# Row maxima of a cross-attention kernel turned in 32 by 32 blocks on VectorE

## The reference: what is computed

```python
x = residual + mha(layernorm(x), layernorm(ctx), W_qkv, b_qkv, W_o, b_o)   # 8 heads of 64, 4096 queries, 3202 keys
  # scores = q @ k.T / 8 ; attn = softmax(scores) ; out = attn @ v ; out @ W_o.T + b_o
xn = layernorm(x)
U = (xn @ W_in.T + b_in) @ Bmat
s = silu(s @ A.T) + u_t                    # scan over the 4096 tokens, state of 64
x = x + states @ Cmat + (program_probs.mean(axis=1) @ W_prog.T + b_prog)
```

## Time and profile before

| | |
|---|---|
| median of 3 runs | 2271.17 us |
| the profiled execution, its own time | 2271.68 us |
| its span, from first to last instruction | 2269.6 us |
| TensorE (PE) busy | 2225.6 us, 98% |
| VectorE (DVE) busy | 1714.8 us, 76% |
| GpSimd (POOL) busy | 1584.3 us, 70% |
| ScalarE (ACT) busy | 1093.8 us, 48% |
| mean granted TensorE clock | 0.993 of full speed |

### The profile page before, as it was taken

The page is one execution under the profiler, slowest core; times in us unless marked ns, Lnnn a source line. Parts: engine busy times, 40 slices in busy tenths (PEclk is TensorE's granted clock), DMA queues, the critical chain, the costliest instruction groups (busy, mean ns, idle before and its releaser), DMA issues.

```text
span 2269.6 us, 36015 instructions
## 1 busy us (share of the span) xinstructions
PE 2225.6 (98%) x14120; PEld 1283.7 (57%) x14120; DVE 1714.8 (76%) x2087; ACT 1093.8 (48%) x1418; POOL 1584.3 (70%) x1038
## 2 busy tenths in 40 slices
PE   8999999999999999999999999999999999999987
PEld 8998865455555555555555555555555555545764
DVE  6866546888888888888888888888888888854766
ACT  4653334545444444444454444444444444453454
POOL 1200027888888888888888888888888888988322
PEclk9999999999999999999999999999999999999998
DMA  7750226777777777777777777777777777778733
GB/s 270 209 184 10 75 76 138 160 157 157 160 157 160 160 168 170 170 165 170 166 156 167 170 173 168 173 173 166 154 158 161 163 173 166 174 178 188 247 103 148
DMA packets 170090, 365.44 MB, mean 161 GB/s; under 512 B 28537, under 2 KB 75001, under 8 KB 169410
## 3 DMA queue, kind: packets, MB, share of 16 engines
q0 software_dynamic: 59904, 218.13, 47.1%
q1 hardware_dynamic: 110018, 145.02, 20.2%
HBM read 95.82 MB, written 49.04 MB: 64 GB/s over the span
## 4 chain that ended last, share of the span: by engine, by line
PE 96%; ACT 1%; DMA 1%; DVE 1%; issue 0%; POOL 0%; SPq 0%; POOLq 0%; DVEq 0%; ACTq 0%
PE ps L1473 34%; PE ps L1338 12%; PE ps L1452 8%; PE ps L1450 8%; PE ps L1454 8%; PE ps L1442 5%; PE ps L1301 4%; PE ps L1540 4%; PE ps L1309 3%; PE ps L1319 3%; PE ps L1273 1%; PE ps L1563 1%; PE ps L1483 1%; PE ps L1343 1%; DMA acca<-pt 1%; PE ps L1603 1%
## 5 line engine op out<-in xcount | busy, mean ns | idle before, releaser
L797 ACT ACTIVATE pt<-ps 128x1024 f32<-128x1024 f32 x800 | 777.5, 1021 | 890.9 <-PE ps L1454 882.2
L1001 DVE TENSOR_REDUCE mx_part<-ps 128x2 f32<-128x1024 f32 x768 | 938.3, 1222 | 339.2 <-PE ps L1338 339.2
L604 POOL TENSOR_TENSOR accp<-accp,pt 128x1024 f32<-128x1024 f32 x416 | 1034.1, 2486 | 209.4 <-ACT pt L797 204.6
L1473 PE MATMUL ps<-pt,v 128*64 128x512 f32 x3328 | 805.8, 605 | 0.0
L1090 DVE TENSOR_TENSOR ps<-ps,shb 128x1024 f32<-128x1024 f32 x403 | 493.2, 1224 | 46.0 <-PE ps L1454 46.0
L1473 PEld LDWEIGHTS ps<-pt,v 128*64 128x64 f32 x3328 | 201.9, 136 | 344.9 <-issue 338.8
L1338 PE MATMUL ps<-kk,qh 64*128 64x512 f32 x1520 | 344.6, 449 | 1.6 <-DVE mx_part L1001 1.6
L1338 PEld LDWEIGHTS ps<-kk,qh 64*128 64x128 f32 x1520 | 141.7, 183 | 341.0 <-DVE mx_part L1001 250.2
L1450 PE MATMUL ps<-qh,kk 64*128 64x512 f32 x1664 | 328.6, 390 | 1.7 <-ACT pt L797 1.7
L1452 PE MATMUL ps<-qh,kk 64*128 64x512 f32 x1664 | 329.0, 390 | 0.0
L1454 PE MATMUL ps<-ql,kk 64*128 64x512 f32 x1664 | 328.3, 389 | 0.0
(11 more groups left out here) (165 smaller groups left out, 1794.2 us busy)
## 6 DMA issues: line engine op xcount, KB each, us to landing
acca<-pt POOLq DMA_DIRECT2D x224, 512.0 KB, 5.0
accb<-pt POOLq DMA_DIRECT2D x160, 512.0 KB, 4.8
q_scratch<-kk SPq DMA_DIRECT2D x32, 512.0 KB, 4.3
acca<-accp POOLq DMA_DIRECT2D x32, 512.0 KB, 4.6
o_scratch<-ost SPq DMA_DIRECT2D x32, 512.0 KB, 3.1
og<-o_scratch SPq DMA_DIRECT2D x32, 512.0 KB, 5.9
shb<-m_scratch SPq DMA_DIRECT2D x31, 512.0 KB, 4.5
xs<-x SPq DMA_DIRECT2D x16, 512.0 KB, 6.1
```

Source lines behind the costliest of these rows:

```text
L604: nc.gpsimd.tensor_tensor(acc[:, :], acc[:, :], pt[n % PT_SLOTS][:, :], ALU.add).then_inc(added_p, 1)
L797: nc.scalar.activation(pt[n % PT_SLOTS][:, :], src, ACT.Exp, scale=SCALE).then_inc(exped, 1)
L1001: nc.vector.tensor_reduce(mx_part[w % 2][:, m % QT, :, m // QT], ps[:, b:b + 2, :], AX_X, ALU.max)\
L1473: ins = mm(ps[HD * h:HD * (h + 1), 6, :], v[:, t, f:f + HD], pt[n % PT_SLOTS][:, h * QB:(h + 1) * QB], start=(t == 0), stop=(t == NT - 1))
```

## The change

The 8 columns are turned on VectorE, in blocks of 32 by 32. `mx_row` becomes 128 by 32 (24 columns are cleared once), and behind the reduction VectorE waits for it and transposes into `mx_turn`; block i (partitions 32i to 32i + 31) then holds 8 rows of 32 queries. SP stores these with four DMAs, one for each block, each of 8 rows of 32 numbers (128 bytes), where one DMA stored 8 rows of 512 bytes. The transpose on TensorE, the copy on ScalarE and their semaphores are gone; the sign moves into `ones_row` (minus one) and into `add_shift` (subtract). `spread_sum` waits for `den_taken` instead, and TensorE waits for `max_taken` before unit 0.

```diff
-        mx_row = at("mx_row", [P, 2, QT], RR + 11776)
+        mx_row = at("mx_row", [P, 32], RR + 11840, F32R)
+        mx_turn = at("mx_turn", [P, 32], RR + 11872, F32R)
-        shift_row = at("shift_row", [2 * QT, P], RR + 11840, F32R)
             def send_shift(w):
-                sp.wait_ge(shift_ready, w + 1)
+                sp.wait_ge(max_ready, w + 1)
                 wait(sp, sh_loaded, 16 * (w - 1))
                 wait(sp, shb_loaded, 16 * (w - 2))
-                sp.dma_start(m_scratch[w % 2].rearrange("h (q k) -> (h q) k", k=P), shift_row[:, :].bitcast(F32)).then_inc(sh_stored, 16)
-                sp.wait_ge(sh_stored, 16 * (w + 1))
+                by_tile = m_scratch[w % 2].rearrange("h (q k) -> (h q) k", k=P)
+                for i in range(4):
+                    sp.dma_start(by_tile[:, 32 * i:32 * (i + 1)], mx_turn[32 * i:32 * i + 2 * QT, :].bitcast(F32)).then_inc(sh_stored, 16)
+                sp.wait_ge(sh_stored, 64 * (w + 1))
-            nc.gpsimd.memset(ones_row[0:1, :].bitcast(F32), 1.0)
+            nc.gpsimd.memset(ones_row[0:1, :].bitcast(F32), -1.0)
...
-            def shift(w):
-                act.wait_ge(max_turned, w + 1)
-                wait(act, sh_stored, 16 * w)
-                nc.scalar.activation(shift_row[:, :], ps[0:2 * QT, turn_bank(w), 0:P], ACT.Copy, scale=-1.0)\
-                    .then_inc(shift_ready, 1)
...
             def take_max(w, m):
                 if m == 0:
-                    wait(dve, max_ready, w - 1)
+                    wait(dve, row_ready, w - 1)
...
             def row_max(w):
+                if w == 0:
+                    dve.wait_ge(row_cleared, 1)
                 dve.wait_ge(max_taken, NM * (w + 1) if w else M_EARLY)
-                wait(dve, max_turned, w)
-                nc.vector.tensor_reduce(mx_row[:, :, :].rearrange("p h q -> p q h"), mx_part[w % 2][:, :, :, :], AX_X, ALU.max)\
-                    .then_inc(max_ready, 1)
+                nc.vector.tensor_reduce(mx_row[:, 0:2 * QT].rearrange("p (h q) -> p q h", h=2), mx_part[w % 2][:, :, :, :], AX_X, ALU.max)\
+                    .then_inc(row_ready, 1)
+                dve.wait_ge(row_ready, w + 1)
+                wait(dve, sh_stored, 64 * w)
+                nc.vector.transpose(mx_turn[:, :].bitcast(F32), mx_row[:, :].bitcast(F32)).then_inc(max_ready, 1)
                     if n == 9:
                         dve.wait_ge(parts_loaded, 32)
+                        nc.vector.memset(mx_row[:, :].bitcast(F32), 0.0).then_inc(row_cleared, 1)
-                nc.vector.tensor_tensor(ps[:, b:b + 2, :], ps[:, b:b + 2, :], shb[u % 2][:, :, :], ALU.add)\
+                nc.vector.tensor_tensor(ps[:, b:b + 2, :], ps[:, b:b + 2, :], shb[u % 2][:, :, :], ALU.subtract)\
                     .then_inc(shifted, 1)
-            def turn_max(w):
-
-                pe.wait_ge(max_ready, w + 1)
-                wait(pe, den_taken, w - 1)
-                if w == 0:
-                    pe.wait_ge(n_ready, 2 * NG)
-                nc.tensor.transpose(ps[0:2 * QT, turn_bank(w), 0:P], mx_row[:, :, :].rearrange("p h q -> p (h q)"), ident[:, :])\
-                    .then_inc(max_turned, 1)
             project_v(NG - 1, 0)
-            turn_max(0)
             project_v(NG - 1, 1)
             pe.wait_ge(k_ready, FC * C_G)
-            pe.wait_ge(shift_ready, 1)
+            pe.wait_ge(max_taken, M_EARLY)
             def spread_sum(u):
                 pe.wait_ge(added_a[u % 2], 16 * (len(A_TILES) + 1) * (u // 2 + 1))
-                if u + 1 < UNITS:
-                    pe.wait_ge(shift_ready, u + 2)
+                wait(pe, den_taken, u)
-                    if ahead and j == TURN_STEP:
-                        turn_max(u + 1)
```

More of the change, by code:

```diff
@@ L55, in maxima_of @@
     return [(i // NM, i % NM) for i in range(first, min(first + 2, NM * UNITS))]
-TURN_STEP = NJ - M_LEAD
 PAIR_ORDER = [2, 3, 0, 1]
@@ L138, in max_bank @@
     return 5 if (w, m) in EARLY else 4
-def turn_bank(w):
-    return 7 if w else 0
 def k_slot(w):
@@ L338, in build @@
         max_done = sem("max_done"); max_taken = sem("max_taken"); max_ready = sem("max_ready")
-        max_turned = sem("max_turned"); shift_ready = sem("shift_ready"); qx_loaded = sem("qx_loaded"); sh_loaded = sem("sh_loaded")
+        row_cleared = sem("row_cleared"); row_ready = sem("row_ready"); qx_loaded = sem("qx_loaded"); sh_loaded = sem("sh_loaded")
         scored = sem("scored"); sh_stored = sem("sh_stored"); shb_loaded = sem("shb_loaded")
@@ L575, in _ @@
             nc.gpsimd.memset(pad[0:KEYS - (NT - 1) * P, :], 0.0)
-            nc.gpsimd.memset(ones_row[0:1, :].bitcast(F32), 1.0)
-            nc.gpsimd.memset(ones_row[HD:HD + 1, :].bitcast(F32), 1.0).then_inc(ones_set, 1)
+            nc.gpsimd.memset(ones_row[0:1, :].bitcast(F32), -1.0)
+            nc.gpsimd.memset(ones_row[HD:HD + 1, :].bitcast(F32), -1.0).then_inc(ones_set, 1)
             pool.wait_ge(ones_set, 2)
@@ L768, in _ @@
                 high_k(C_G - 1, i)
-            shift(0)
             for t in range(GT):
@@ L823, in _ @@
                         high_o(u - 1)
-                    if j == TURN_STEP and u + 1 < UNITS:
-                        shift(u + 1)
                     if u == UNITS - 2 and j in (3, 5, 7, 9):
```

## The result

The changed kernel takes 2258.89 us, the median of 4 runs (2256.72 to 2263.44), against 2271.69 us beside it: ratio 0.9948, 95% interval 0.9937 to 0.996. Timed again with six runs it gave 0.9958 (0.9946 to 0.997). The forecast was 2258.4 us in a range of 2257 to 2265.

The account below looks back on a forecast made before the run. The prediction took TensorE to bound the kernel: 12.5 us from steps 9 plus 0.3 us before unit 0, 12.8 us off 2271.68, gave 2258.9, or 2258.4 us against the median of the runs, range 2257 to 2265.

Parts of the forecast that it names:

- What bounds: Whole kernel: TensorE holds 96% of the chain of waits, so time is saved where TensorE issues or waits less.
- TensorE in steps 9, 12.5 us: Removing 31 transposes gives 0.41 us in each of 30 steps 9 and 0.20 us in the last, 12.5 us.
- the hand-over of the banks: Step 9, before the second piece of maxima: 0.10 us might be lost each time; none taken, 3 us kept for the range.
- What follows moves as a block: The attention and what follows it shift together, since TensorE releases what follows; no loss was counted there.
- In front of unit 0, 0.3 us: Without transpose and ScalarE copy, the first copy of v starts 0.29 us earlier; gain 0.3 us.
- rival C: Steps 9: only the transpose's own 0.20 us is won, 6.5 us in all, giving 2264.7 us; chance 0.04.
- VectorE: Added wait of 0.04 us and transpose of 0.20 us per unit hide in 0.9 us of slack; nothing, up to 3 us.
- SP: Four stores of maxima for one, 0.9 us more issue time but begun earlier; nothing, with 2.6 us of room before unit 0.
- Rival A: VectorE's transpose is held until GpSimd's sum ends, delaying step 9's second piece; 2291.4 us against the median, chance 0.11.
- B: Another chain, denominators' accumulating DMAs or VectorE's hand-over, holds TensorE and the gain is given back; about 2271 us, chance 0.06.

Follow-up runs that it names:

- e1: The changed kernel with the TensorE transpose put back in its old places, its result read by nobody; 2270.85 us, ratio 0.9998 to the kernel before.
- e6: The changed kernel with a ScalarE copy of 8 by 64 put back at the old copy's places, output unread; 2263.17 us, ratio 0.9966.
- e2: The changed kernel without VectorE's second wait, on row_ready, before a unit's first piece of maxima; 2260.3 us, ratio 0.995.
- e5: The kernel before with its TensorE transpose moved within step 9, behind the second piece of maxima and directly ahead of pv; 2263.84 us, ratio 0.9963.
- e9: The changed kernel with two SP loads, in units 28 and 31, moved behind the denominators' DMAs of the same unit; 2258.42 us, ratio 0.9952.
- e10: The changed kernel with one single TensorE transpose, in step 9 of unit 30, read by nobody; 2260.23 us in one run.
- e3: The changed kernel with a 128 by 32 float32 VectorE copy behind the transpose in all units but the first, output unread; 2287.95 us, ratio 1.0073.

## Why the prediction was right

**What bounds.** Right. e1 turns the whole gain off by TensorE's instruction alone, and e6's units show that ScalarE's was worth nothing.

**TensorE in steps 9, 12.5 us.** The mechanism was right, the size too large. Each step gave 0.37 us by the medians, not 0.41: 30 x 0.37 + 0.2 = 11.3 us. I had named the hand-over of the banks, kept up to 0.10 us a step for it in the range and taken none. It took 0.05, and e2 shows where most of it arises: in the second wait ahead of VectorE's reduction, which was there before as well, hidden while the transpose was longer. The Trainium skill's duration for the transpose ("TensorE: Matmul & The Clock Gate", Part 4), taken as the price, gave 8.5 us, further from the 11.3 of the steps than 12.5 was. A difference from step to step was the better measure, and e5 shows why: 0.25 us go with the instruction, 0.16 with its place.

**What follows moves as a block.** This is the sentence that failed, for 2 to 3 us. In units 28 and 31, SP's large loads stand beside the accumulating DMAs. There an accumulating DMA takes 8 to 10 us (4.9 is the median of all), and ScalarE waits. From the trace of the changed kernel, ScalarE in unit 28:

```profile
1862.47 1.02 ACT L784 ACTIVATE pt<-ps 128x1024 f32<-128x1024 f32 x1 [2.31 <-DMA acca<-pt]
```

The kernel before had such waits in unit 31 too, and in its second trace one period longer by 1.2 us in unit 29. In the changed kernel unit 28 is longer in all three traces, by 0.8 to 1.5 us, and the last unit takes 1.6 us more. Part of the 1.6 us is the clock: at full clock throughout the last unit took 77.0 us before and 78.1 after (one trace each), with a stretch at half 77.6 before and 79.4 and 79.1 after. So 1.1 us are there at full clock too.

e9 shows that the loads make the wait in unit 28 and most of those in unit 31. Why they cost more in the changed kernel stays open, since e10's one turn did not bring the old length back and e6's ScalarE copy did not either. The earlier loads of `sh` alone are not it, since e1 has them and has a last unit of 77.5 us. The traces show one thing more of unit 28: with the loads in their old place all six traces with a period of about 54.4 us have ScalarE's wait there (1.5 to 2.3 us), and none of the five with a period of 54.6 us or more has it (the two of before, e1, e5, e3). e3 lacks the transpose on TensorE too, so the wait goes with the shorter unit and not with the missing instruction; through which chain isn't shown.

**In front of unit 0, 0.3 us.** Right: between the first group of v matmuls and the second lie 0.69 us where 0.95 lay (318.18 less 317.23). The trace of before held 1.6 us more there, a half clock, which I read as the length of the group without looking at its clock. Part of the 12.4 us between the two spans is that, and it hid the loss at the end.

**The number.** That the time came out within 0.5 us of the forecast is in part luck. One term was 1.2 us too large and 2 to 3 us of losses were not foreseen, and against them stand outer stages that move by 3 us with the clock. Executions at the same mean granted clock of 0.995 took 2258.75 to 2261.05 us with the change (three) and 2270.5 us on the mean before (eleven): about 11 us, where I had 12.8. One figure of the prediction is a slip: rival C stands at 2264.7 us against the median, as its own sum says, and not at 2264.2; it stays inside the range.

**VectorE.** Right: 0.21 us for the 0.20 taken, 0.89 us of slack left. **SP.** Right in the outcome, with four issues at 1.96 us together where I took 1.2; the slack covers it. In front of unit 0 TensorE used `sh` at 320.31 and not at 322.6, in good part because the clock was at full, so there was less than the 2.6 us of room I had counted. Nothing on the path waited for `sh`, there or in the units.

**Rival A** was a true mechanism on the wrong instruction. e3 prices it: with an instruction of the kind that is held in that place, the kernel is 0.7% slower, 2287.95 us for the 2291.4 I had reckoned. The lock that the Trainium skill describes ("SBUF — State Buffer", section "SBUF: two separate sides") is seen in the copy, which ends 0.03 us behind GpSimd's sum; the transpose, with one input and float32 as well, is not held in any of the 31 units that have a sum beside it. Rival **B** came true in small, in two units. **C** did not: the piece fell from 0.43 to 0.27 us.

## What to carry to other kernels

Where TensorE bounds, price an instruction there by the distance from one step to the next with and without it, not by its duration; and look at what stands on either side: moving the transpose by two places, directly ahead of other instructions over 128 rows, gave 0.16 of the 0.37 us a step and a kernel of 2263.84 us, with no other change. Before putting work into an idle gap of VectorE beside a busy GpSimd, find out whether that instruction is of the kind that is held: a copy here cost 0.90 us a time and a transpose of the same size nothing. A gain of fractions of a microsecond a step can be partly given back at the few places where a large load meets a chain of DMAs, so look for those before summing. And where differences are a few microseconds, compare runs of a like granted clock: executions of the changed kernel at 0.992 took about 4 us more than those at 0.995.

## What the runs showed of the hardware

- A float32 transpose of 128 by 32 on VectorE takes 211 to 214 ns, SBUF to SBUF, in 31 units with a GpSimd sum running and in front of unit 0 with none. A float32 copy of the same size ended 35 to 44 ns behind the sum in 31 of 31 cases and took 1.30 to 1.98 us.
- Four DMA issues of 8 rows of 128 bytes took 1.30 us on SP in front of unit 0 and 1.96 us in unit 12, where one of them took 0.93; the issue of 8 rows of 512 bytes took 0.29.
- The transpose on TensorE cost 0.41 us in its first place and 0.25 us directly ahead of `pv` (steps 9 of 4.55 and 4.39 us, where step 10 takes 4.14).
- The granted clock fell to half for 3.4 us at about 312 us of the span in four of thirteen traces, one of them without a transpose there; twelve v matmuls then took 4.59 us for 3.03.
- Accumulating DMAs of 512 KB, 4.9 us in the median, took 8 to 10 us beside SP's loads of 256 KB and of 2 MB.
- A second wait ahead of a VectorE instruction, long satisfied, delayed its start by 0.07 us (0.61 us behind the matmuls against 0.54 in e2).
